# The last twelve steps of a token stage, written out in another order

## The reference

```python
x = x + xattn(layernorm(x), ctx, Wq, Wk, Wv, Wo, bo)        # 8 heads of 64, 64 context rows of 384
x = x + ffn(layernorm(x), gate_w, bias, W1, W3, W2, sw1, sw3, sw2)
# ffn: X is (16384, 512)
scores = sigmoid(X @ gate_w.T)                              # 32 experts
_, idx = top_k(scores + bias, 4)
w = scores[idx] / sum(scores[idx])
pos = rank of the token among those of its expert, in token order; valid = pos < 512
xe[e, pos] = X[token]                                       # where valid
ye = (silu(xe @ W1) * (xe @ W3)) @ W2                       # per expert, 256 hidden
out = sum over the 4 experts of ye[e, pos] * w  +  (silu(X @ sw1.T) * (X @ sw3.T)) @ sw2.T
```

## Time and profile before

| | |
|---|---|
| time of three runs | 1948.73, 1951.99 (median), 1953.79 us |
| profiled execution | 1951.55 us; its span is 1949.7 us |
| busy share of the span | PE 90%, DVE 82%, POOL 64%, PEld 64%, ACT 38% |
| mean granted TensorE clock | 0.961 |
| token stage | from 0 to 1468.4 us, when POOL does its first instruction of the expert stage |

### The profile page before, as it was taken

The page is one execution under the profiler, slowest core; times in us unless marked ns, Lnnn a source line. Parts: engine busy times, 40 slices in busy tenths (PEclk is TensorE's granted clock), DMA queues, the critical chain, the costliest instruction groups (busy, mean ns, idle before and its releaser), DMA issues. The chain is left out here.

```text
span 1949.7 us, 31394 instructions
## 1 busy us (share of the span) xinstructions
PE 1747.2 (90%) x9424; PEld 1243.4 (64%) x9424; DVE 1591.0 (82%) x4143; ACT 748.8 (38%) x1253; POOL 1241.8 (64%) x1107
## 2 busy tenths in 40 slices
PE   6898899999999999999999999999732999999991
PEld 4775567777777767777776777776411556555551
DVE  5887789999999999999999999999821777676671
ACT  3343334444444444344443444443301444444440
POOL 2235566666676666667666666666675577888864
PEclk8998999999999999999999999999975999999995
DMA  7339987764446464444545444554326799999976
GB/s 210 99 103 101 100 131 131 127 142 119 118 125 145 118 140 132 118 116 132 141 121 139 122 119 121 130 139 111 91 55 204 171 232 218 226 232 220 226 140 78
DMA packets 335195, 275.00 MB, mean 141 GB/s; under 512 B 199858, under 2 KB 242098, under 8 KB 335028
## 3 DMA queue, kind: packets, MB, share of 16 engines
q1 hardware_dynamic: 289972, 203.48, 44.0%
q0 software_dynamic: 45056, 69.52, 18.6%
HBM read 134.07 MB, written 105.25 MB: 123 GB/s over the span
## 5 line engine op out<-in xcount | busy, mean ns | idle before, releaser
L640 POOL DMA_INDIRECT slot_table<-tok,slot x512 | 514.9, 1006 | 125.7 <-issue 121.1
L658 POOL TENSOR_TENSOR xt_l<-xt,xt_h 128x512 fp32r<-128x512 f32 x128 | 166.1, 1298 | 181.8 <-PE S_ps L374 118.5
L1099 POOL DMA_INDIRECT out<-ye,idx x128 | 205.2, 1603 | 88.4 <-issue 37.2
L390 PE MATMUL O_ps<-m_h,pt_h 128*128 128x512 f32 x512 | 217.7, 425 | 33.7 <-issue 30.8
L1251 DVE TENSOR_TENSOR xe_l<-TE_ps,xe_h 128x512 f16<-128x512 f32 x128 | 88.4, 691 | 168.5 <-issue 87.3
L374 PE MATMUL S_ps<-a_h,xt_h 128*128 128x512 f32 x512 | 200.9, 392 | 7.2 <-POOL xt_l L658 7.2
L390 PE MATMUL O_ps<-m_h,pt_l 128*128 128x512 f32 x512 | 201.3, 393 | 0.0
L374 PE MATMUL S_ps<-a_h,xt_l 128*128 128x512 f32 x512 | 201.1, 393 | 0.0
L374 PE MATMUL S_ps<-a_l,xt_h 128*128 128x512 f32 x512 | 200.6, 392 | 0.0
L390 PE MATMUL O_ps<-m_l,pt_h 128*128 128x512 f32 x512 | 200.2, 391 | 0.0
L651 POOL TENSOR_TENSOR ht_l<-hid,ht_h 128x512 fp32r<-128x512 f32 x64 | 82.8, 1294 | 181.2 <-ACT ht_h L622 181.1
(11 more groups left out here) (175 smaller groups left out, 4837.6 us busy)
## 6 DMA issues: line engine op xcount, KB each, us to landing
xt<-in_xT SPq DMA_DIRECT2D x128, 256.0 KB
xr<-in_x SPq DMA_DIRECT2D x64, 512.0 KB, 3.9
x2aug<-x SPq DMA_DIRECT2D x128, 256.0 KB
out<-xr SPq DMA_DIRECT2D x64, 512.0 KB
up_w<-in_w SPq DMA_DIRECT2D x64, 256.0 KB
slot_table<-tok,slot POOLq DMA_INDIRECT x512
down_raw<-in_w SPq DMA_DIRECT2D x32, 256.0 KB
x2t_h<-x_h SPq DMA_TRANSPOSE x128
```

The source lines that it names most:

```text
L390: last = pe.matmul(O_ps[:, :], left[:, p * P:(p + 1) * P], right[:, b % 2, p, :], start=(m == 0), stop=(m == 3 * PAIRS - 1))
L640: pool.indirect_dma_start(table, bass.IndirectOffsetOnAxis(ap=slot[:, g % 2, i, q:q + 1], axis=0), tok[:, t:t + 1], None, bounds_check=SLO ...
L658: pool.tensor_tensor(xt_l[:, :, :], xt[:, :, :], xt_h[:, t % 2, :, :].bitcast(F32), ALU.subtract).then_inc(xt_lo, 1)
L1099: pool.indirect_dma_start(out, bass.IndirectOffsetOnAxis(ap=idx[:, e, c:c + 1], axis=0), ye[:, e % 4, c, :], None, bounds_check=TOKENS + P ...
```

## The change

Only the end of the token stage changes; up to step 134 nothing does, save for two semaphores in place of one for the transposes (`x2_turned`, by odd and even tiles).

- `rows_at(n)` takes the place of `at(n, X2)`: step 134 has tile 121, step 135 tiles 122 and 123, step 136 none, step 137 tiles 124 and 125, step 138 tiles 126 and 127. From tile 125 on the odd tiles have parts of their own, laid over the buffer `xt`, which is no longer read then (`row_parts`, `parts_free`).
- `logits_at(n)`: tiles 122 and 123 in step 136, tiles 124 to 127 together in step 139.
- `routed_at(n, lag)`: group 30 is routed one step earlier and group 31 two steps earlier: slots of group 30 in step 138, of group 31 in step 141. The FFN steps of the groups stay.
- `filed_at(n)`: tiles up to 119 as before; then 120 and 121 in step 139 (beside 119), 122 and 123 in step 140, 124 and 125 in step 141, 126 and 127 in step 142. In a step POOL files two of the four experts for each tile and then the other two for each.
- From step 136 on DVE runs `late_step`: members and slots first, then X1 with its statistics, pt_l, the weights, all 13 root operations in a row (those of the last pair in step 137, not 138), the lower parts of the rows, the routing, the ranks, and the FFN last.
- The lower parts `ht_l` of groups 30 and 31 are computed by DVE (`hidden_lo`) and no longer by POOL (`HELD` = 30).
- `STEPS` is 146.

```diff
 X_LOAD, LN1_STATS, ROOTS, XT_LOAD, XT_SPLIT, SCORES, MIX, X1 = 2, 4, 6, 6, 7, 8, 9, 10
 X2, LOGITS, FFN_UP, FFN_DOWN = 13, 14, 17, 19
 ROUTE, MEMBERS, SLOTS_AT, WEIGHTS, OUT, W_STORE, TABLE = 17, 18, 19, 20, 20, 21, 20
-STEPS = TILES - 4 + TABLE + 4
+LAST = TILES - 4
+LATE = LAST + 12
+HELD = GROUPS - 2
+STEPS = LAST + 22
 NEWTON = 12
 LATER = 3
...
+
+def rows_at(n):
+
+    if n < LAST + X2 - 2:
+        return [n - X2] if n >= X2 else []
+    return {LATE - 1: [LAST - 2, LAST - 1], LATE + 1: [LAST, LAST + 1], LATE + 2: [LAST + 2, LAST + 3]}.get(n, [])
+
+
+def logits_at(n):
+
+    if n < LATE + 2:
+        return rows_at(n - 1)
+    return [LAST, LAST + 1, LAST + 2, LAST + 3] if n == LATE + 3 else []
+
+
+def filed_at(n):
+
+    t = n - TABLE
+    normal = [t] if 0 <= t < LAST - 4 else []
+    pair = 2 * (n - LATE - 3)
+    return normal + ([LAST - 4 + pair, LAST - 3 + pair] if 0 <= pair < 8 else [])
+
+
+def routed_at(n, lag):
+
+    for sooner in range(3):
+        g = GROUPS - 3 + sooner
+        if n == 4 * g + lag - sooner:
+            return g
+    g = group_at(n, lag)
+    return g if g is not None and g < GROUPS - 2 else None
 
...
             return (PREP_ps, U_ps, G_ps, O_ps, U_ps, G_ps, O_ps, U_ps)[j]
+
+        def row_parts(t):
+            if t > LAST and t % 2:
+                both = xt[:, :, :].rearrange("p c t -> p (c t)").bitcast(F16)
+                return both[:, 0:D], both[:, D:2 * D]
+            return x2_h[:, :], x2_l[:, :]
+
+        def parts_free(eng, t):
+            if t == LAST + 1:
+                eng.wait_ge(xt_lo, TILES)
+            elif t > LAST:
+                eng.wait_ge(x2_turned[t % 2], t // 2 * 32)
+            elif t:
+                eng.wait_ge(x2_turned[(t - 1) % 2], ((t - 1) // 2 + 1) * 32)
...
                     q = pair_at(n, X_LOAD)
                     if q is not None and q >= 4:
                         load_tokens(q // 2, q % 2)
-                    g = group_at(n, W_STORE)
+                    g = routed_at(n, W_STORE)
                     if g is not None:
                         sp.wait_ge(w_ready, g + 1)
                         sp.dma_start(w_groups[g][:, :, D:ROW], wfull[:, g % 2]).then_inc(w_stored[g % 2], 16)
-                    t = at(n, X2)
-                    if t is not None:
+                    for t in rows_at(n):
                         sp.wait_ge(x2_done, t + 1)
                         sp.dma_start(x2_tiles[t][:, 0:D], x2[:, t % 2, :]).then_inc(x2_stored[t % 2], 16)
                         g, i = t // 4, t % 4
                         after(sp, u_done, g * 4 - 6)
-                        for n_lo, part, turned in ((x2_hi, x2_h, x2t_h), (x2_lo, x2_l, x2t_l)):
+                        for n_lo, part, turned in zip((x2_hi, x2_lo), row_parts(t), (x2t_h, x2t_l)):
                             sp.wait_ge(n_lo, t + 1)
-                            sp.dma_start_transpose(turned[:, g % 2, :, i * P:(i + 1) * P], part[:, :]).then_inc(x2_turned, 16)
+                            sp.dma_start_transpose(turned[:, g % 2, :, i * P:(i + 1) * P], part).then_inc(x2_turned[t % 2], 16)
                     t = at(n, XT_LOAD)
...
+                    pe.wait_ge(x2_turned[t % 2], (t // 2 + 1) * 32)
                     if i == 0:
                         after(pe, lexp_done, g)
-                    if i == 1:
+                    if i == 1 or g == GROUPS - 1:
                         after(pe, rank_read, g)
...
-                    t = at(n, LOGITS)
-                    if t is not None:
+                    for t in logits_at(n):
                         logits(t)
                     bp, q = kv_job(n)
                     if bp is not None:
...
                             dst = m_h[:, b % 2, j - KD, :]
                         act.activation(dst, prep_bank(b, j)[:, :], ACT.Copy).then_inc(prep_hi, 1)
 
-                    t = at(n, X2)
-                    if t is not None:
+                    for t in rows_at(n):
                         q = t // 2
                         act.wait_ge(scaled, q + 1)
                         after(act, x2_lo, t - 1)
-                        after(act, x2_stored[t % 2], t // 2 * 16)
-                        act.activation(x2[:, t % 2, :], x_tile(t), ACT.Identity,
-                                       bias=nb2[:, q % 2, t % 2:t % 2 + 1],
+                        after(act, x2_stored[t % 2], q * 16)
+                        act.activation(x2[:, t % 2, :], x_tile(t), ACT.Identity, bias=nb2[:, q % 2, t % 2:t % 2 + 1],
                                        scale=rs[:, (q + LATER) % 2, 1, t % 2:t % 2 + 1]).then_inc(x2_done, 1)
                         act.wait_ge(x2_done, t + 1)
-                        after(act, x2_turned, t * 32)
-                        act.activation(x2_h[:, :], x2[:, t % 2, :], ACT.Copy).then_inc(x2_hi, 1)
+                        parts_free(act, t)
+                        act.activation(row_parts(t)[0], x2[:, t % 2, :], ACT.Copy).then_inc(x2_hi, 1)
 
                     t = at(n, XT_SPLIT)
...
@@ -644,20 +687,22 @@
                 def step(n):
                     for c in range(2):
                         g = group_at(n, FFN_UP + c + 1)
-                        if g is not None:
+                        if g is not None and g < HELD:
                             pool.wait_ge(ht_hi, g * 2 + c + 1)
                             after(pool, g_done, g * 4)
                             after(pool, u_done, g * 4)
                             pool.tensor_tensor(ht_l[:, c, :], hid[:, :], ht_h[:, c, :].bitcast(F32),
                                                ALU.subtract).then_inc(ht_lo, 1)
-                    file(at(n, TABLE), 0, 2)
+                    for t in filed_at(n):
+                        file(t, 0, 2)
                     t = at(n, XT_SPLIT)
                     if t is not None:
                         pool.wait_ge(xt_hi, t + 1)
                         after(pool, scores_done, t)
                         pool.tensor_tensor(xt_l[:, :, :], xt[:, :, :], xt_h[:, t % 2, :, :].bitcast(F32),
                                            ALU.subtract).then_inc(xt_lo, 1)
-                    file(at(n, TABLE), 2, TOP)
+                    for t in filed_at(n):
+                        file(t, 2, TOP)
                     t = at(n, SCORES)
                     if t is not None:
...
+                def hidden_lo(g, c):
+                    dve.wait_ge(ht_hi, g * 2 + c + 1)
+                    dve.wait_ge(u_done, g * 4)
+                    dve.tensor_tensor(ht_l[:, c, :], hid[:, :], ht_h[:, c, :].bitcast(F32), ALU.subtract).then_inc(ht_lo, 1)
+
+                def rows_lo(t):
+                    dve.wait_ge(x2_hi, t + 1)
+                    parts_free(dve, t)
+                    dve.tensor_tensor(row_parts(t)[1], x2[:, t % 2, :], row_parts(t)[0], ALU.subtract).then_inc(x2_lo, 1)
+
+                def late_step(n):
+                    s9, s10 = at(n, MIX), at(n, X1)
+                    early, members = routed_at(n, ROUTE), routed_at(n, MEMBERS)
+                    slots, weights = routed_at(n, SLOTS_AT), routed_at(n, WEIGHTS)
+                    if members is not None:
+                        route_mark(members)
+                        route_count(members)
+                        route_before(members)
+                        route_member(members)
+                    if slots is not None:
+                        slot_place(slots)
+                        slot_spread(slots)
+                        slot_list(slots)
+                    if s10 is not None:
+                        dve.wait_ge(o_done, s10 + 1)
+                        dve.tensor_tensor(x_tile(s10), x_tile(s10), O_ps[:, :], ALU.add).then_inc(x1_done, 1)
+                        dve.wait_ge(x1_done, s10 + 1)
+                        after(dve, agg2, s10 - 3)
+                        dve.bn_stats(st2[:, s10 % 4, :], x_tile(s10)).then_inc(bn2, 1)
+                        aggregate2(s10)
+                    if s9 is not None:
+                        dve.wait_ge(pt_hi, s9 + 1)
+                        dve.tensor_tensor(pt_l[:, :], TP_ps[:, :], pt_h[:, :].bitcast(F32), ALU.subtract).then_inc(pt_lo, 1)
+                    if weights is not None:
+                        for k in range(5):
+                            weigh_ops(weights, k)
+                    for k in range(NEWTON + 1):
+                        if n == LATE:
+                            roots(n, k)
+                        elif n == LATE + 1:
+                            roots(n + 1, k)
+                    for t in rows_at(n):
+                        rows_lo(t)
+                    if early is not None:
+                        route_scores(early)
+                        route_sigmoid(early)
+                        route_bias(early)
+                        route_best(early)
+                        route_cut(early)
+                    if members is not None:
+                        slot_over(members)
+                        slot_rank(members)
```

(29 more changed lines are left out.)

9 lines of the change are left out of this document (3 added, 6 removed).

## The result

The kernel before took 1948.73 us (median of 21 runs beside the changed one), the changed kernel 1958.82 (21 runs): ratio 1.0051, 95% interval 1.0039 to 1.0063. It is 10 us slower, where 1944.9 was forecast, with a range of 1940.8 to 1951.5. The profiled execution of the changed kernel has a span of 1956.5 us against 1949.7.

A forecast was written before the change was run, and what follows sets the result against it. POOL's queue was taken to bound the token stage: 15.5 us off it, less late starts in step 135, a 3.7 us wait for group 30's slots and 0.5 of collisions, gains 7.1: 1951.99 to 1944.9 us, range 1940.8 to 1951.5.

The forecast's parts named there:

- What bounds the kernel: End of the token stage: POOL's queue sets the end; its last filing ends 6.96 us before the expert stage.
- What comes off POOL: Four subtractions and their waits for ht_h go to DVE; POOL would end 15.5 us earlier if nothing else held it.
- Step 135: x2_h of tile 123 ahead of pt_h: DVE's attention for the last two tiles 4.5 us late, POOL's multiply 4.1.
- PE hardly matters: In the chain to group 30's slots: a mix needs 3.1 us from the end of pt_l to X1.
- Slots of group 30: DVE's chain from X1 of tile 126 takes 20.9 us, so POOL waits 3.7 us after 14 filings.
- rival B: A stall like the old 5.15 us one falls into the new DVE run: gain 2.0, 1950.0 us; chance 0.11.
- What must not come later than POOL: Group 31's slots at 1428.6, asked for at 1433.6, reserve 5 us; FFN and stores end within POOL's cover.
- The sum: The expert stage shifts whole: 1951.99 less 7.1 gives 1944.9 us; chance of this case 0.55.
- rival A: The 5.15 us stall before X1 of tile 127 is not in ordinary executions: gain 2.6, 1949.4 us; chance 0.14.
- Rival D: DVE subtractions beside POOL's filings all collide at the SBUF port: gain 3.8, 1948.2 us; chance 0.04.
- Rival E: DVE's run of dependent late_step operations takes half as long again, 31.4 us: slower, 1955.3 us; chance 0.08.
- Rival C: DVE's chain is shorter and POOL never waits: gain 10.8, 1941.2 us; chance 0.08.

The follow-up runs named there:

- e3: Changed kernel with the four subtractions ht_l of groups 30 and 31 back on POOL; 1944.05 us, ratio 1.0094 to the kernel before.
- e5: Changed kernel with only group 31's subtractions ht_l on DVE, group 30's back on POOL; 1937.10 us, ratio 1.0051 to the kernel before.
- e1c: Changed kernel without the 48 filings of tiles 116 to 127, in an execution with late increments; 1929.40 us, kernel before 1952.61.
- e8: Changed kernel with tile 123's row after the attention and eight POOL pauses until filings landed, late increments elsewhere; 1943.83 us, ratio 0.9990 to before.
- e9: Changed kernel with tile 123's row after the attention and five POOL pauses, execution without late increments; 1933.12 us, ratio 0.9998 to before.
- e6b: Changed kernel with tile 123's row after the attention in step 135, execution with late increments; 1961.30 us, ratio 1.0039 to before.
- e2b: Changed kernel with a POOL memset in place of each of the 48 filings, late increments elsewhere; 1921.80 us, kernel before 1946.71.

## Why the prediction was wrong

**What bounds the kernel.** Right. POOL's queue sets the end in both kernels: 6.95 us from the last filing to the expert stage, and 6.96 in the earlier trace rows.

**What comes off POOL.** Right: no subtraction and no wait for ht_h is left, and e3 and e5 show that without this part the new order is 9 to 14 us longer.

**Step 135.** Forecast 4.5 us late for the maxima, measured 4.2 to 4.7 over all executions with this step. It failed where the chain goes on, at "PE hardly matters": another 1.4 us (1.5 in the profile of the result) went to a mix at the lower clock.

**Slots of group 30.** The forecast had 20.9 us of chain; 20.7 to 20.9 were measured in prompt executions, so the count of DVE's operations was right. In the profiled execution of the result it was 27.6: 3.46 and 3.07 us of waits for PE's increments. This is the mechanism of rival B, "such a stall falls into the new DVE run", which I priced at 5.15 once and 0.11.

**"What must not come later than POOL".** This is the step that failed and cost most. Slots(31) were forecast at X1 + 39.1 with 5 us in reserve, by a chain in which a late increment of PE was put at nothing; they came at X1 + 59.8. Of the 20.7 us, 6.7 came with group 30. Then ACT's exponential took the logits 5.5 us after their last matmul (1421.74 to 1427.27), and DVE stood idle 2.29 and 5.59 us for residuals. In the changed kernel's prompt executions the list comes at 38.0 to 38.8, and in the late ones without unbroken filings, e1c and e8, at 37.5 and 38.5. The FFN's last residual, which starts at X1 + 80.6, went the same way, and stayed covered by a POOL that was itself late.

**The sum, late.** In the tail: 4.7 at step 135, 1.5 in the mix, 4.6 after X1, together 10.7, as measured. The forecast had a gain of 11.6 after X1 (7.1, and the 4.5 of step 135 regained); POOL ended 16.2 later than drawn, which makes the loss of 4.6. In the 16.2, the waits for lists have 18.0 (21.7 beyond the usual 0.30 between filings, for 3.7); off it go 1.5 for a first filing that is earlier relative to X1 and 0.3 for collisions that cost 0.2 and not 0.5.

**The sum, prompt.** 7.1 forecast; 4.7 of it never was there, because before loses its gap as well (rival A, which gave 2.6); 1.4 more goes to the mix. That leaves a gain of 1.0, and the tails give 0.9 in one pair of executions and -0.2 in the other. Rivals A and B were one thing seen from two sides: the gap goes with the kind of the execution, and it was longer beside the longer runs of the changed kernel. I gave it two separate chances, each with the 5.15 us of the one row that I had. The argument against A, that the profiled time equals the median, could not tell them apart, since executions run together share a kind. That the changed kernel is 10 us slower, and not equal, hangs on the kind that it met.

**Rival D**, the port collisions (SBUF — State Buffer page of the Trainium skill, "Who interferes with whom"), did not show: the 48 filings of the changed kernel have a mean of 984 ns as the 39 of the earlier trace rows have 991, and the longest in the timeline are 1.09 and 1.08 us. Half of the 8 subtractions ran while POOL stood still; beside the other four, the filings took 0.98 us but for the one of 1.09. **Rival E**, the chain of small operations taking longer by itself, is excluded by the prompt runs; its time, 1955.3, was near the result for another reason. **Rival C** did not occur.

**Open.** Why some executions have the late increments, and why indirect DMAs of POOL bring them out, is not shown; the kind could not be chosen, and none of the experiments looks inside. The kind touches more than PE: in the late executions close to a fifth of the semaphore updates of every computing engine is missing from the trace (it has 3601 to 3671 for 4396 of DVE's, and 1100 to 1127 for 1328 of PE's), where the prompt ones have nearly all (4383 to 4407, and 1328 to 1336). Yet only PE's are seen to be late. Whether the recording itself has a part in it, no run tells. Nor is a long run of filings needed for every gap: four late executions have one of 1.5 to 3.2 us ahead of an X1 near 206 us, after only two filings. Neither before without filings nor e9 met a late execution, so how much of before's own tail is due to it there (4.7 to 5.5 us by the difference of its tails) rests on comparing executions. No version was found that gains in both kinds.

## What to carry to other kernels

Read a single idle gap that no releaser explains as a question about everything near it, and ask what it would cost if it came each time that pattern comes; the pattern was there to see: a run of indirect DMAs that ended 1.9 us before the gap did, and a second engine held up at the same place. When a reordering lays a chain that hops between engines beside a longer unbroken run on another queue, each hop is a place for such a delay, and a count of operations doesn't see it. And an operation put ahead of a feeder of PE can cost twice, as here: once by its wait and once by the clock at which PE resumes. Repeat the kernel before as well as the changed one: here its tail alone differed by 5 us between the kinds, about as much as the best version gained.

## What the runs showed of the hardware

- In some executions semaphore increments of PE come up to 13.4 us (first profile, 1425.05 to 1438.47) and 17.0 us (e6b) after the matmul's end while POOL issues indirect DMAs every 1.284 us, with DMA engines 2% busy. The longest delays of the first profile end about 2 us after the filings stop, others during them, and some increments are not held up. No wait for DVE, ACT or POOL was seen to be held up so. Without the filings (e1c), with memsets in their place (e2b), or with waits for landing between them (e8), the tail has none.
- Such executions are slower elsewhere too: the expert stage, which the change does not touch, takes 478.0 to 483.5 us in place of 468.1 to 471.5, whatever the version.
- Waiting until the last filing of POOL has landed takes 1.9 to 2.8 us.
- After 5.5 to 5.9 us without matmuls PE resumed at a granted clock of 0.50 in all 12 executions that had such a gap ahead of the mix, and its 12 matmuls took 4.3 to 5.4 us; after 1.2 to 1.3 us it kept 1.00 in the 8 others, and they took 3.0.
